# Second expert layer turned round: features on the partitions, 512 tokens moving, and the token weights read back from DRAM

## The reference, cut to what matters

```python
logits = x @ gate_weight.T
probs = softmax(logits)
topv, topi = top_k(probs, 8)
...                                   # small ones dropped, the rest made to sum to 1
combine = zeros((T, 32)).at[arange(T)[:, None], topi].add(routing_weights)

def expert_step(acc, xs):
    w_gu, w_d, c_e = xs
    g, u = split(x @ w_gu.T, 2, axis=-1)
    h = silu(g) * u
    return acc + h @ w_d.T * c_e[:, None], None
out = scan(expert_step, zeros_like(x), (gate_up_proj, down_proj, combine.T))
x = layernorm(x + out)
```

## Time and profile before

| | us |
|---|---|
| median of three runs | 672.63 |
| lowest, highest | 671.83, 681.43 |
| span of the profiled execution, first to last instruction | 627.6 |
| PE busy in the span | 555.8 |
| PE weight load busy | 481.3 |
| DVE busy | 354.2 |
| ACT busy | 237.4 |
| POOL busy | 269.0 |
| PE, stretch of 394.35 to 616.00 | 221.60 of 221.65 |

### The profile page before, as it was taken

The page is one execution under the profiler, slowest core; times in us unless marked ns, Lnnn a source line. Parts: engine busy times, 40 slices in busy tenths (PEclk is TensorE's granted clock), DMA queues, the critical chain, the costliest instruction groups (busy, mean ns, idle before and its releaser), DMA issues.

```text
span 627.6 us, 11175 instructions
## 1 busy us (share of the span) xinstructions
PE 555.8 (89%) x3453; PEld 481.3 (77%) x3453; DVE 354.2 (56%) x970; ACT 237.4 (38%) x617; POOL 269.0 (43%) x257
## 2 busy tenths in 40 slices
PE   8999985099989999989887778899999999999994
PEld 4666675078879889866444566899999999999994
DVE  4636686636664444338999566664444443444445
ACT  4645542245546665336020142233332333323234
POOL 3484024778987877602787600004042240404000
PEclk9979997589999999989998797899999999999998
DMA  8999891255876676400000420002020202000001
GB/s 259 372 387 384 284 333 52 105 177 168 232 225 188 192 237 185 133 0 1 1 1 0 152 75 2 0 1 70 8 77 2 76 0 75 0 0 0 0 0 67
DMA packets 58605, 70.93 MB, mean 113 GB/s; under 512 B 5681, under 2 KB 53570, under 8 KB 58562
## 3 DMA queue, kind: packets, MB, share of 16 engines
q10 hardware_dynamic: 35968, 35.26, 16.9%
q1 hardware_dynamic: 19234, 26.18, 13.4%
q0 software_dynamic: 3360, 8.93, 4.5%
HBM read 36.02 MB, written 34.34 MB: 112 GB/s over the span
## 4 chain that ended last, share of the span: by engine, by line
PE 67%; DVE 11%; DMA 5%; issue 4%; POOL 3%; ACT 3%; ACTq 1%; DVEq 0%; POOLq 0%
PE PS L1746 47%; DMA FA<-xg 5%; PE PS L2040 3%; POOL xg L662 3%; DVE FA L1700 2%; PE PS L1970 2%; DVE PS L1682 2%; PE PS L2065 2%; PE PS L2176 1%; PE PS L1821 1%; PE PS L1843 1%; PE PS L2089 1%; PE PS L2188 1%; PE PS L1983 1%; PE PS L1806 1%
## 5 line engine op out<-in xcount | busy, mean ns | idle before, releaser
L1746 PE MATMUL PS<-EW,XH 128*128 128x384 f32 (+3 forms) x764 | 215.4, 364 | 6.7 <-DVE SQ L1485 3.1
L1746 PEld LDWEIGHTS PS<-EW,XH 128*128 128x128 f32 x764 | 131.4, 193 | 11.9 <-DVE SQ L1485 3.4
L1485 DVE SCALAR_TENSOR_TENSOR SQ<-SIL,CW,PS 128x96 f32<-128x96 f32 x256 | 69.0, 311 | 116.6 <-ACT SIL L918 115.8
L1746 PE MATMUL PS<-EW,XL 128*128 128x384 f32 (+3 forms) x382 | 133.6, 350 | 0.0
L1746 PE MATMUL PS<-EW,EHH 128*128 128x256 f32 (+1 forms) x476 | 102.3, 290 | 0.2
L918 ACT ACTIVATE SIL<-PS 128x192 f32<-128x192 f32 x128 | 42.6, 332 | 158.0 <-PE PS L1746 158.0
L1746 PE MATMUL PS<-EW,EHL 128*128 128x256 f32 (+1 forms) x286 | 80.4, 281 | 0.0
L1746 PEld LDWEIGHTS PS<-EW,EHH 128*128 128x128 f32 (+1 forms) x476 | 78.5, 189 | 1.4 <-issue 0.6
L629 POOL TENSOR_TENSOR round_mark<-round_mark 128x1 f32<-128x1 f32 x10 | 1.9, 194 | 175.0 <-PE PS L1746 167.9
L1746 PEld LDWEIGHTS PS<-EW,XL 128*128 128x128 f32 x382 | 73.2, 192 | 2.1
L1746 PEld LDWEIGHTS PS<-EW,EHL 128*128 128x128 f32 (+1 forms) x286 | 54.0, 189 | 0.0
(11 more groups left out here) (373 smaller groups left out, 1048.5 us busy)
## 6 DMA issues: line engine op xcount, KB each, us to landing
xg<-EQ ACTq DMA_DIRECT2D x1, 16384.0 KB, 61.3
EG<-in_gateup SPq DMA_DIRECT2D x16, 448.0 KB, 4.1
yg<-EQ ACTq DMA_DIRECT2D x1, 6016.0 KB, 20.4
FA<-xg ACTq DMA_DIRECT2D x47, 128.0 KB, 2.9
yg<-FA ACTq DMA_DIRECT2D x47, 128.0 KB, 3.0
ED<-in_down SPq DMA_DIRECT2D x16, 224.0 KB, 4.7
EG<-in_gateup SPq DMA_DIRECT2D x4, 768.0 KB, 4.5
FA<-in_gateup SPq DMA_DIRECT2D x4, 768.0 KB, 4.6
```

The costliest lines, as they stand in the source:

```text
L1485: ins = dve.scalar_tensor_tensor(out=HH[:, pos % 2, h:h + W], in0=SIL[:, s, j * W:(j + 1) * W], scalar=c, in1=bank(s)[:, I + j * W:I + (j ...
L1746: ins = pe.matmul(o, l, r, start=start and i == 0, stop=stop and i == n - 1, skip_group_check=True)
```

## The change

The second expert layer is computed the other way round. The weights are stationary, 128 hidden features of a quad at a time, and 512 tokens move; so gate and up come out with the features on the partitions, as down needs them. A quad has 384 features, 3 chunks, and the tokens have 2 halves: 6 steps in a quad, 48 in all (`step_of`). Gate and up of a step are 12 matmuls of 512 columns into two banks, down is 12 of 256 columns.

- The turns between are gone. ACT applies silu over 512 elements. In the first 6 steps (`AHEAD`) ACT copies up out of PSUM and POOL multiplies; from then on DVE multiplies silu by up, straight from PSUM. The result, `mixed`, waits in one of 13 buffers.
- A token's weight is now a number for each column, the same for all 96 partitions of an expert. So the whole of CW is made first (`combine`: six operations on 1,024 elements), TensorE turns it with 8 transposes after step 5, ACT and DVE copy it, SP stores it to DRAM (`cw_room`), and for every step SP reads the rows of its two experts back, each spread over its partitions with 2 DMAs, into one of 4 buffers (`load_spread`). POOL multiplies `mixed` by it, ACT rounds, DVE takes the low part from two operands in SBUF.
- Down of a step comes ten steps after its gate and up (`LAG`). ACT and DVE do the parts nine steps after.
- The router has the tokens on the partitions from the start: X stationary, 64 columns move, 32 matmuls, and DVE adds the parts in one reduction. Gate and up of the first steps do not wait for the routing. The residual stands ahead of the router.
- The gate load of a quad is four DMAs of 768-byte pieces instead of one of 3,072-byte pieces; POOL's splits are cut into halves and spread over the steps (`next_split`), and they and the loads wait for gate and down apart. SP issues the loads of quad k+4 between the spreads.
- The last norm is done in two halves (`layernorm_halves`), the first after the step that closes tokens 0 to 511.
- All 48 steps are written out, without a hardware loop. Some semaphores are joined.

On TensorE, at the layer's start before the change: the router (L2002, L2008), the residual (L2015) and the first matmul of the first unit (L1746).

The core of the diff:

```diff
+CHUNKS = 3
+QUADS = E1 // QUAD
+STEPS = QUADS * 2 * CHUNKS
+LAG = 10
+AHEAD = 6
+MIXED, SPREADS, TURNED = 13, 4, 3
...
+    def load_gate(q):
+        if q >= 2:
+            sp.wait_ge(gate_split, q - 1)
+        land = quad_slot(q)[0].rearrange("p (k g a i) -> p k g a i", k=KD, g=2, a=QUAD // PAIR)
+        for k in range(KD):
+            rows = a["gateup1"][q, k * P:(k + 1) * P, :].rearrange("p (a g i) -> p g a i", a=QUAD // PAIR, g=2)
+            for up in range(2):
+                sp.dma_start(land[:, k, up], rows[:, up]).then_inc(gate_ld[q % 2], 16)
+    def load_down(q):
+        if q >= 2:
+            sp.wait_ge(down_split, q - 1)
+        sp.dma_start(quad_slot(q)[3].rearrange("p (c d) -> p c d", d=D),
+                     a["down1"][q].rearrange("(c p) d -> p c d", p=P)).then_inc(down_ld[q % 2], 16)
+    def load_spread(i):
+        q, hf, c = step_of(i)
+        if i >= SPREADS:
+            sp.wait_ge(weighted, i - SPREADS + 1)
+        first = c * P // I1
+        cut = (first + 1) * I1 - c * P
+        for e, rows in ((first, slice(0, cut)), (first + 1, slice(cut, P))):
+            sp.dma_start(spread_w[i % SPREADS][rows, :],
+                         cw_room[q * QUAD + e:q * QUAD + e + 1, hf * BANK:(hf + 1) * BANK].broadcast_to(
+                             [rows.stop - rows.start, BANK])).then_inc(spread_ld[i % SPREADS], 16)
+    sp.wait_ge(exp_split, MOE.E)
+    load_gate(0)
+    load_down(0)
+    sp.wait_ge(s_done, DV1)
+    for q in range(1, 4):
+        load_gate(q)
+        load_down(q)
+    sp.wait_ge(cw_step, CW_COPIED)
+    sp.dma_start(cw_room, cw_turned).then_inc(cw_stored, 16)
+    sp.wait_ge(cw_stored, 16)
+    for i in range(STEPS):
+        load_spread(i)
+        q = i // 6 + 4
+        if i % 6 == 2 and q < QUADS:
+            load_gate(q)
+        q = (i - 11) // 6 + 4
+        if i >= 11 and i % 6 == 5 and q < QUADS:
+            load_down(q)
...
+    def next_split(i):
+        at, j = divmod(i, 2 * CHUNKS)
+        q = at + 1
+        if 2 <= q < QUADS:
+            g, gh, gl, _, _, _ = quad_slot(q)
+            if j == 0:
+                pool.wait_ge(gate_up_mm, 2 * 2 * CHUNKS * (q - 1))
+                pool.wait_ge(gate_ld[q % 2], 32 * KD * (q // 2 + 1))
+                rounded["g0"] = high(gh, g, half(0))
+            if j == 2:
+                low(gl, g, gh, half(0), rounded["g0"])
+            if j == 3:
+                rounded["g1"] = high(gh, g, half(1))
+            if j == 4:
+                low(gl, g, gh, half(1), rounded["g1"]).then_inc(gate_split, 1)
+        q = at - 1
+        if 2 <= q < QUADS:
+            _, _, _, d, dh, dl = quad_slot(q)
+            if j == 0:
+                pool.wait_ge(dn_done, 2 * CHUNKS * (q - 1))
+                pool.wait_ge(down_ld[q % 2], 16 * (q // 2 + 1))
+                rounded["d"] = high(dh, d, whole)
+            if j == 1:
+                low(dl, d, dh, whole, rounded["d"]).then_inc(down_split, 1)
+    rounded = {}
+    for i in range(STEPS + LAG - 1):
+        if i < AHEAD:
+            pool.wait_ge(sil_done, i + 1)
+            pool.wait_ge(up_copied, i + 1)
+            pool.tensor_tensor(mixed[:, i % MIXED, :], sil_t[:, i % 2, :], up_t[:, i % 2, :], ALU.mult
+                               ).then_inc(mixed_pool, 1)
+        v = i - (LAG - 1)
+        if v >= 0:
+            if v < AHEAD:
+                pool.wait_ge(mixed_pool, v + 1)
+            else:
+                pool.wait_ge(mixed_dve, v - AHEAD + 1)
+            pool.wait_ge(spread_ld[v % SPREADS], 32 * (v // SPREADS + 1))
+            pool.tensor_tensor(mixed[:, v % MIXED, :], mixed[:, v % MIXED, :], spread_w[v % SPREADS], ALU.mult
+                               ).then_inc(weighted, 1)
+        next_split(i)
...
+    def moe_act():
+        for i in range(STEPS + LAG - 1):
+            if i < STEPS:
+                b = step_bank(i)
+                act.wait_ge(gate_up_mm, 2 * i + 1)
+                if 2 <= i < AHEAD + 2:
+                    act.wait_ge(mixed_pool, i - 1)
+                elif i >= 2:
+                    act.wait_ge(mixed_dve, i - 1 - AHEAD)
+                act.activation(sil_t[:, i % 2, :], bank(b), ACT.Silu).then_inc(sil_done, 1)
+                if i < AHEAD:
+                    act.wait_ge(gate_up_mm, 2 * i + 2)
+                    act.activation(up_t[:, i % 2, :], bank(b + 1), ACT.Copy).then_inc(up_copied, 1)
+                if i == AHEAD - 1:
+                    act.wait_ge(cw_step, CW_TURNED)
+                    act.activation(cw_turned[:, 0:BANK], bank(2)[0:E1, :], ACT.Copy).then_inc(cw_step, 1)
+            v = i - (LAG - 1)
+            if v >= 0:
+                act.wait_ge(weighted, v + 1)
+                if v >= TURNED:
+                    act.wait_ge(dn_done, v - TURNED + 1)
+                act.activation(h_hi[:, v % TURNED, :], mixed[:, v % MIXED, :], ACT.Copy).then_inc(h_hi_done, 1)
...
-        dve.wait_ge(rt_mm, 2)
...
+        dve.wait_ge(rt_mm, 1)
+        dve.tensor_reduce(lg, bank(0).rearrange("p (t s e) -> p t e s", t=NT, s=2), AX_X, ALU.add
+                          ).then_inc(rt_read, 1)
+        dve.wait_ge(rt_read, 1)
+        ch.link(dve.tensor_reduce(rsum[:], lg, AX_X, ALU.max))
+        dve.tensor_tensor(lg, lg, col(rsum[:], E), ALU.subtract).then_inc(rt_max, 1)
...
+    def moe_dve():
+        dve.wait_ge(cw_step, CW_TURNED)
+        dve.tensor_copy(cw_turned[:, BANK:2 * BANK], bank(3)[0:E1, :]).then_inc(cw_step, 1)
+        for i in range(AHEAD, STEPS + LAG - 1):
+            if i < STEPS:
+                dve.wait_ge(sil_done, i + 1)
+                dve.wait_ge(gate_up_mm, 2 * i + 2)
+                if i >= MIXED:
+                    dve.wait_ge(h_lo_done, i - MIXED + 1)
+                dve.tensor_tensor(mixed[:, i % MIXED, :], sil_t[:, i % 2, :], bank(step_bank(i) + 1), ALU.mult
+                                  ).then_inc(mixed_dve, 1)
+            v = i - (LAG - 1)
+            if v >= 0:
+                dve.wait_ge(h_hi_done, v + 1)
+                dve.tensor_tensor(h_lo[:, v % TURNED, :], mixed[:, v % MIXED, :], h_hi[:, v % TURNED, :].bitcast(F32),
+                                  ALU.subtract).then_inc(h_lo_done, 1)
...
-        for hf in range(2):
-            pe.wait_ge(lo_done, tp * (NT // 2) + 2 * (hf + 1))
+        for t in range(NT):
+            if t % 2 == 0:
+                pe.wait_ge(lo_done, tp * (NT // 2) + t // 2 + 1)
             for i in range(2 * KD):
-                ins = pe.matmul(bank(hf)[0:2 * WRC, :], WRS[:, i // 2, :],
...
+                k = i // 2
+                both = WRS[:, k, :].rearrange("p (s e) -> p s e", s=2)[:, :, c:c + E]
+                ins = pe.matmul(bank(0)[:, t * 2 * E:(t + 1) * 2 * E].rearrange("p (s e) -> p s e", s=2),
+                                (XH, XL)[i % 2][:, k, t * P:(t + 1) * P], both,
+                                start=(t == 0 and i == 0), stop=(i == 2 * KD - 1), skip_group_check=True)
...
+    def moe_pe():
+        def gate_up(i):
+            q, hf, c = step_of(i)
+            b = step_bank(i)
+            if i % (2 * CHUNKS) == 0:
+                pe.wait_ge(gate_split, q + 1)
+            before = bank_before(i)
+            if i == 0:
+                pe.wait_ge(lo_done, 4 * (NT // 2))
+            elif i == 1:
+                pe.wait_ge(rt_read, 1)
+            elif i == AHEAD + 1:
+                pe.wait_ge(cw_step, CW_COPIED)
+            else:
+                pe.wait_ge(sil_done, before + 1)
+            _, gh, gl, _, _, _ = quad_slot(q)
+            for up in range(2):
+                if up and i >= 2 and i != AHEAD + 1:
+                    if before < AHEAD:
+                        pe.wait_ge(up_copied, before + 1)
+                    else:
+                        pe.wait_ge(mixed_dve, before - AHEAD + 1)
+                lhs = [(chunk_of(gh, k, up, c), chunk_of(gl, k, up, c)) for k in range(KD)]
+                mm3(bank(b + up), lhs, xm(hf), True, True).then_inc(gate_up_mm, 1)
+        def turn_weights():
+            pe.wait_ge(cw_step, CW_READY)
+            pe.wait_ge(sil_done, AHEAD - 1)
+            pe.wait_ge(up_copied, AHEAD - 1)
+            for t in range(NT):
+                ins = pe.transpose(bank(2 + t // 4)[0:E1, t % 4 * P:(t % 4 + 1) * P], CW[:, t, :], ident[:])
+            ins.then_inc(cw_step, 1)
+        def down(i):
+            q, hf, c = step_of(i)
+            if i % (2 * CHUNKS) == 0:
+                pe.wait_ge(down_split, q + 1)
+            pe.wait_ge(h_lo_done, i + 1)
+            _, _, _, _, dh, dl = quad_slot(q)
+            cols = slice(c * D, (c + 1) * D)
+            for t in range(HALF):
+                p = slice(t * P, (t + 1) * P)
+                ins = mm3(pair_bank(hf * HALF + t), [(h_hi[:, i % TURNED, p], h_lo[:, i % TURNED, p])],
+                          [(dh[:, cols], dl[:, cols])], False, True)
             ins.then_inc(dn_done, 1)
-        run_units(pe, m, gate_up, [(turn, 1), (down, 2)])
-        pe.wait_ge(dn_done, base + m.total)
```

(10 more changed lines are left out.)

381 lines of the change are left out of this document (147 added, 234 removed).

## The result

| | before | after |
|---|---|---|
| median of four runs beside each other, us | 672.23 | 647.63 |
| lowest, highest | 669.88, 681.43 | 643.65, 648.65 |
| span of the profiled execution | 627.6 | 646.5 |

The ratio is 0.9619, with a 95% interval of 0.9576 to 0.9662: faster, by 24.6 us where 31.3 were forecast (647.6 against 641.0, range 634 to 657).

What follows compares the result with a forecast made beforehand. TensorE was taken to bound the second expert layer. Turns 21.1, wide matmuls 2.1, residual, router and waiting 7.1 and the end 1.2 make 31.5, taken as 31.3 off 672.6: 641 us, range 634 to 657.

Steps and rivals of the forecast that it cites:

- The bound and the large term: Second expert layer: TensorE sets its time, and removing the 192 turns between matmuls gains 21.1 us.
- case 1: Whole kernel stays TensorE-bound as forecast, 636 to 647 us, with DVE-POOL meetings costing none to 5.2; chance 0.57.
- cases 2 to 4: POOL and SP's loop of loads and spreads bounds: 650 to 659 (0.17), 659 to 686 (0.12), over 686 us (0.05).
- case 5: Whole kernel better than forecast: wide matmuls nearer 0.222 us and no meetings, under 636 us; chance 0.09.
- The start of the stage: After the transposes: residual ends at 381.3, router at 384.8, step 5 at 401.5 us; weights ready at 403.6.
- the meetings of DVE and POOL: In the combine, four clashes between DVE and POOL operations delay the weights 2.0 us, or 5.2 by the skill's rule.
- The pitch of down: In the loop, down's 256-column matmuls take 0.118 us each, making a step 4.19 us.
- The last downs: At the layer's end, downs run at TensorE's pace of 1.41 us each, the last ending at 588.9 us.
- The way of the weights back: Store, read back and product after the turns are ready 3.4 us before the first down; the lag hides it all.
- The ring of POOL and SP: Loop of splits, loads and spreads takes 22 to 24 us a quad, 25.3 with meetings, against 25.1; costs 0 us.
- The tail: After the last down, the norm in two halves saves about 1.2 of 8.6 us, leaving 7.4.
- The 45 us around the span: Runs' median 672.63 against profiled span 627.6: 45.0 us lie outside the span and were left unchanged.

Runs made afterwards that it cites:

- spreads_two: The changed kernel with two buffers instead of four for the weights read back; 197.08 us from the turns to the end, against 197.6 to 197.7.
- defer: The changed kernel with POOL's six early products waiting for CW, silu and up kept in free `mixed` buffers; ratio to before 0.9542.
- after_third: The changed kernel run again without an edit, beside joined_two on one chip; ratio to before 0.9588.
- joined_two: Changed kernel: POOL's early products behind CW, router before residual, last down split later, first-half statistics earlier, ACT writing that half's four tiles; ratio to before 0.9542.
- after_again: The changed kernel run again without an edit, on another occasion; ratio to before 0.9590.

## Why the prediction was right, point by point

**The bound and the large term hold.** TensorE 150.00 of 150.00 busy; no turn between matmuls but eight; gate and up of steps 0 to 5 in 16.80 us (427.43 to 444.23), 2.80 each; behind the transposes TensorE's only wait of more than half a microsecond is the one ahead of the eight turns, with DVE's CW as its releaser. That the 21.1 us of turns would be gained was the core of the forecast, and the layer's 23.9 hold it: 48 steps of 4.22 are 202.6 us where 64 units took 224.1, a gain of 21.5. No experiment takes the turns away alone.

**The rivals.** 647.6 stands just above the upper end of case 1 (636 to 647), whose mechanism it is, with the meetings near the 5.2 that this case allowed. None of the others took place: no spread waited for by TensorE (cases 2 to 4), and no wide matmul nearer to 0.222 (case 5).

**The start of the stage holds to 0.2 us** up to the end of step 5, the router's pitch of 0.11 and the halved clock in the residual included. The clock's part is partly luck: the residual took 4.85 us here and 3.62 in spreads_two, with the same work ahead.

**The step that failed is the meetings of DVE and POOL.** I took four at 0.5, 2.0 us in all, only in the combine, from the DVE operation of 1.09 beside POOL and the POOL one of 1.83 beside DVE. Measured were five waits on DVE: 0.72, 0.92 and 1.00 in small operations of the routing that I had given none, and 0.98 and 0.95 in the combine. The rows that the price of 0.5 came from have a short partner each: DVE's operation at 9.82 stood behind a POOL rounding of 0.62, and POOL's of 1.83 behind a DVE operation of 0.68. In the timelines of before:

```profile
9.76 0.62 POOL L606 TENSOR_SCALAR EW<-FA 128x512 fp32r<-128x512 f32 x1
```

```profile
346.57 0.68 DVE L1707 TENSOR_TENSOR FA<-FA,QT 128x512 f32<-128x512 f32 x1
```

In after the partner is POOL's product of 1.3, and a wait is up to twice as long. The five waits are 4.6 us, and since steps and CW would have met within 0.1 us, TensorE waited 4.53 for them. In the combine my 2.0 came out (1.93, as two waits of nearly 1 and not four of 0.5); the 2.6 that I missed are the three small operations. defer shows it: without the products beside them every one of the five is back at its own length. The Trainium skill, page "SBUF — State Buffer", section "Who interferes with whom", says that the one that comes first takes the port pair that DVE and GpSimd share for its whole instruction while the other is blocked, and names `tensor_scalar` in its two-port mode beside the operations with two inputs in SBUF; those are the kinds that waited here. The trace agrees with it in kind: POOL's product at 439.44 took 2.21 and L1553 behind it 2.20. The 5.2 us that I had worked out by it were nearer than my 2.0, but partly by luck: they stood for four waits of 1.29 in the combine, and what came were five of 0.72 to 1.00, three of them ahead of it.

**What I left out: the clock behind that wait.** TensorE idles 4.5 us and then runs at 1.2 GHz for a while (granted clock 0.52 from 448.76 to 452.30, 1.00 behind); the turns took 1.5 instead of 0.9 and the first step after them another 1.0. defer, in which there is no wait, takes 1.5 less from the turns on. The fall does not follow every wait: after one of 2.4 us the turns took 1.9 in after_third and 1.05 in spreads_two.

**The pitch of down** is 0.120 and not 0.118: the rows from 637.81 to 638.77 are eight pitches in 0.96. A step is 4.22, not 4.19, and over 48 steps 1.4 us.

**The last downs.** I took the products on POOL to be hidden to the end. A lone down takes 1.44, a product and a low part that exclude each other 1.7; 1.9 us. Together 2.3 + 0.6 + 1.0 + 1.4 + 1.9 = 7.2 of the 7.3.

**The way of the weights back** held: 3.8 us of reserve for 3.4. Its parts were off in both directions (store 3.9 for 3.1, spreads 3.0 to 3.3 for 2.6), here in after's list of transfers, in the columns of the earlier trace rows:

```profile
HC<-cw_room SPq DMA_DIRECT2D x16, 192.0 KB, 3.0
QT<-cw_room SPq DMA_DIRECT2D x16, 192.0 KB, 3.3
...
cw_room<-WW SPq DMA_DIRECT2D x1, 128.0 KB, 3.9
```

**The ring of POOL and SP** cost nothing, as forecast, but its margin was misjudged. Rivals 2 to 4 had a third of the chance between them because I laid issue, landing and product end to end twice in each quad. Doubling the issues changed nothing that can be seen, and halving the buffers cost 0.9 us, all of it at the very end; POOL works up to nine steps ahead of TensorE's downs, and its waits for spreads (22.9 and 12.3 us in after) are those of an engine that is early. A rounding of half a gate load, taken at 0.74, took 0.84.

```profile
L865 POOL TENSOR_TENSOR FA<-FA,HC 128x512 f32<-128x512 f32 x24 | 34.5, 1445 | 22.9 <-DMA HC<-cw_room 22.9
...
L865 POOL TENSOR_TENSOR FA<-FA,QT 128x512 f32<-128x512 f32 x24 | 34.8, 1455 | 12.3 <-DMA QT<-cw_room 12.3
```

**The tail** came out at 7.45 for 7.4. The reason was only half right: both halves' norms run one after the other on DVE, and joined_two shows that another 1.1 us lay there.

**The 45 us around the span** are a step of the prediction that was wrong and did no harm: they were one short execution set against longer ones. The difference was taken in the layer, which takes 249.9 and 251.1 us in the two profiles of before.

Open: why the stages of the first expert layer take some 40 us more on some occasions; why TensorE ran at 1.2 GHz for a while in steps 0 to 5 in some executions of one kernel (after_third) and not in others (after_again) with the same work ahead; and why its clock fell behind a wait of 2.4 us in one execution and not in another.

## What to carry to other kernels

Where an engine waits for a chain on DVE, look at what POOL does beside it, and count a wait for every DVE operation with two inputs in SBUF, and every `tensor_scalar`, that can meet it, small ones too (here 0.7 to 1.0 us beside products of 1.3); such products should stand behind the chain if their result is not wanted sooner. Work that only fills TensorE (the residual here) belongs behind what another engine is waiting for. And a queue in order that runs far ahead needs care at its end: one early wait (the split for the last quad) pushes all that is behind it into the stretch where nothing hides it.

## What the runs showed of the hardware

- A DVE operation of 8 elements by 128 partitions took 0.89 and one of 64 elements 1.24 beside POOL's product, 0.17 and 0.22 without it.
- The stages ahead of the layer, the same work in all changed kernels, ended between 374 and 427 us, with DMA at 205 GB/s in the one case shown and 152 in the other.
- Between the layer's transposes and the turns TensorE's mean clock was 0.79 to 0.88 in the four kernels without a wait for CW and 0.88 to 0.95 in the eight profiles with one; the one with the lowest was busy 31.92 of 32.76 us. Against after, the edits that take the wait of 4.5 us away gained 1.0 to 2.7 us ahead of the turns at that lower clock, and joined_two none.
- A wait of 4.5 us ahead of the turns was followed by some 3.5 us at 1.2 GHz, 1.6 us lost up to the first down (16.4 against 14.8). Of the waits of 2.4 us, four were followed by it (turns of 1.89 us) and one was not (1.05).
